# Matmuls of an identity in PE's waits at the openings of a mixture of experts and of an attention

## What is computed

```python
x = x + attention0(layernorm(x), ctx, ctx)            # 16 heads of 16, softmax over 64 keys
x = x + expert_choice_ffn(layernorm(x))               # 8 experts, each takes its top 1024 of 8192 rows
x = x + attention1(layernorm(x), ctx, ctx, masks)     # the same, with a key mask and a pad mask
x = x + zone_ffn(layernorm(x))                        # 8 experts of width 256 on every row, weights by a router
```

## Time and profile before

| what | value |
|---|---|
| median of 3 runs | 2336.3 us (2335.57 to 2337.42) |
| the profiled execution, its own time | 2335.41 us |
| its span, first to last instruction | 2333.3 us |
| mean granted clock of PE | 0.968 of 2.4 GHz |
| PE busy | 2171.5 us, 93% of the span |
| DVE, ACT, POOL busy | 1453.1, 872.9, 361.6 us |
| DMA | 114.00 MB, 49 GB/s on the mean |

### The profile page before, as it was taken

One profiled execution on the slowest core, in us unless ns is written; L12 is line 12 of the kernel. 1 busy time (PEld: TensorE's weight loads), 2 busy tenths in 40 slices (PEclk: granted clock), 3 DMA queues, 4 the chain that ended last, 5 costly groups with the idle time before them and its releaser, 6 DMA issues. The chain is left out here.

```text
span 2333.3 us, 40339 instructions
## 1 busy us (share of the span) xinstructions
PE 2171.5 (93%) x15221; PEld 1855.4 (80%) x15221; DVE 1453.1 (62%) x3169; ACT 872.9 (37%) x1245; POOL 361.6 (15%) x347
## 2 busy tenths in 40 slices
PE   6999998638999769999998999999999999999998
PEld 4888887427898747777777888888888888888887
DVE  6888887785555368777776854545545555544444
ACT  2555554124555235555454322222222222222222
POOL 3111110106776411111112100000000000000000
PEclk9999999858999979999999999999999999999999
DMA  3121211104544312112213100000000000000000
GB/s 98 55 72 63 81 63 46 30 3 132 108 102 77 37 37 73 63 54 72 81 64 127 37 15 14 28 28 28 28 28 28 1 28 28 28 28 28 28 10 10
DMA packets 109098, 114.00 MB, mean 49 GB/s; under 512 B 16064, under 2 KB 97728, under 8 KB 108992
## 3 DMA queue, kind: packets, MB, share of 16 engines
q1 hardware_dynamic: 96704, 95.44, 12.8%
q0 software_dynamic: 12288, 17.05, 4.5%
HBM read 61.87 MB, written 50.59 MB: 48 GB/s over the span
## 5 line engine op out<-in xcount | busy, mean ns | idle before, releaser
L2224 DVE TENSOR_TENSOR zmix_hid<-zmix_act_gate,psum 128x1024 f32<-128x1024 f32 x128 | 156.3, 1221 | 378.6 <-issue 350.8
L2180 ACT ACTIVATE zmix_hid_hi<-zmix_hid 128x1024 fp32r<-128x1024 f32 x128 | 135.6, 1059 | 393.6 <-PE psum L144 232.5
L2172 ACT ACTIVATE zmix_act_gate<-psum 128x1024 f32<-128x1024 f32 x128 | 131.4, 1027 | 377.4 <-PE psum L144 377.3
L752 PE MATMUL psum<-att_v_cur,att_probs 128*128 128x96 f32 x2048 | 247.9, 277 | 3.1 <-ACT att_probs L911 3.1
L752 PEld LDWEIGHTS psum<-att_v_cur,att_probs 128*128 128x128 f32 x2048 | 238.1, 192 | 10.9 <-ACT att_probs L911 4.0
L2229 DVE TENSOR_TENSOR zmix_hid_lo<-zmix_hid,zmix_hid_hi 128x1024 fp32r<-128x1024 f32 x128 | 157.8, 1233 | 134.9 <-ACT zmix_hid_hi L2180 133.9
L142 PE MATMUL psum<-zmix_wd_hi,zmix_hid_hi 128*128 128x256 f32 x768 | 217.3, 283 | 2.2 <-DVE zmix_acc L2215 1.9
L143 PE MATMUL psum<-zmix_wd_lo,zmix_hid_hi 128*128 128x256 f32 x768 | 217.2, 283 | 0.0
L144 PE MATMUL psum<-zmix_wd_hi,zmix_hid_lo 128*128 128x256 f32 x768 | 217.1, 283 | 0.0
L2215 DVE SCALAR_TENSOR_TENSOR zmix_acc<-psum,opened_weight,zmix_acc 128x256 f32<-128x256 f32 x512 | 211.7, 476 | 1.6 <-PE psum L144 1.6
L911 ACT ACTIVATE att_probs<-psum 128x512 f32<-128x512 f32 x256 | 132.2, 604 | 144.4 <-PE psum L731 73.7
(11 more groups left out here) (395 smaller groups left out, 5445.2 us busy)
## 6 DMA issues: line engine op xcount, KB each, us to landing
x<-att_x_new SPq DMA_DIRECT2D x32, 512.0 KB, 2.9
att_x_in<-in_x SPq DMA_DIRECT2D x16, 512.0 KB, 3.8
rows<-att_normed_new SPq DMA_DIRECT2D x16, 512.0 KB, 3.0
att_x_in<-x SPq DMA_DIRECT2D x16, 512.0 KB, 3.8
turned<-att_newT SPq DMA_DIRECT2D x16, 512.0 KB, 2.8
zmix_acc<-x SPq DMA_DIRECT2D x16, 512.0 KB, 4.1
out_x<-zmix_acc SPq DMA_DIRECT2D x16, 512.0 KB, 3.2
moe_wd<-in_w_down SPq DMA_DIRECT2D x8, 768.0 KB
```

Source lines behind the costliest of these rows:

```text
L752: m = pe.matmul(psum[:, 6 + t % 2, cols], probs[:, j, t * P:(t + 1) * P], v_cur[:, p, cols], start=True, stop=True)
L2172: act.activation(act_gate[:, :, :], psum[:, 0:2, :], ACT.Silu).then_inc(gate_out, 1)
L2180: act.activation(hid_hi[:, e % 2, :, :], hid[:, :, :], ACT.Copy).then_inc(hi_made, 1)
L2224: dve.tensor_tensor(hid[:, :, :], act_gate[:, :, :], psum[:, 2:4, :], ALU.mult).then_inc(up_out, 1)
```

## The change

A helper issues `times` matmuls of `ident16` against itself, repeated to 512 columns, into bank 7. Nothing reads what they write, and they wait for nothing and signal nothing. It is called at four places of PE's stream: 42 and 10 times at the mixture, 28 times and twice 8 times (a call in a loop of two) at attention 1.

```diff
+def keep_running(pe, const, psum, times):
+
+    for _ in range(times):
+        pe.matmul(psum[:, 7, :], const["ident16"][:, :], const["ident16"][:, :].unsqueeze(1).to_broadcast([P, TT, P]), start=True, stop=True)
@@ attention, PE's stream, the branch of the second attention
             else:
                 pe.wait_ge(cleared, 2)
+                keep_running(pe, const, psum, 28)
                 turn_input(0, 0)
                 pe.wait_ge(mask_ready, 2)
                 masks(0)
                 queries(0, 0)
                 for c in range(KC):
                     maxima(0, 0, c)
+                    keep_running(pe, const, psum, 8)
                 turn_maxima(0)
             batches(pe, body, close)
@@ expert_choice_mixture, PE's stream
+            keep_running(pe, const, psum, 42)
             turn(0, 0, 0)
+            keep_running(pe, const, psum, 10)
             iterations(pe, body)
```

## The result

The changed kernel took 2328.86 us (median of 10 runs, 2327.38 to 2333.44), the kernel before 2337.59 us beside it (10 runs, 2334.78 to 2340.96): a ratio of 0.9967, 95% interval 0.9959 to 0.9976, which of 2336 us is 7.7 us less, with 5.6 and 9.6 as the ends (the two medians themselves lie 8.7 apart). A second series of the same two kernels gave 0.9971 (0.9960 to 0.9983). The forecast of 2330.9 us lies 2.0 us above the first median, and that median is 0.4 us under the lower end of the range. The times of one kernel don't lie evenly: of 35 runs of the kernel before in a later series 20 lie at 2331.2 to 2335.5 and 15 at 2336.6 to 2340.6, so a median of ten moves by a microsecond or two with how many of each it got.

The account below looks back on a forecast made before the run. PE was taken to bound the kernel, busy 2171.5 of 2333.3 us; 2.4 us at the mixture and 3.0 at the second attention gave 2336.3 - 5.4 = 2330.9 us, with an 8-in-10 range of 2329.3 to 2335.0.

Parts of the forecast that it names:

- Price of an idle matmul: Each further added 512-column matmul on PE costs 0.42 us at 1.2 GHz and 0.22 us at 2.4 GHz.
- Climb r: Time from the start of PE's added matmuls until its clock rises: 4.8 to 5.8 us, with 3.3 as an end.
- The 42, 0.8 late: Mixture's opening: the 42 matmuls ahead of the first transposes end 0.8 us after the rows PE waits for.
- Transposes 0.9 and the first up projection 2.3: Mixture's opening: at the risen clock the 8 transposes save 0.9 us and the first 12 matmuls 2.3 us.
- Rival 2: Mixture's opening: another engine takes the pace and the up projection's 2.3 us return as waits; gain 3.1, 2333.2 us; chance 0.21.
- Mixture opening: Mixture's opening as a whole: 0.9 + 2.3 - 0.8 = 2.4 us gained, with ends 3.2 and 2.1.
- The 28 not late: Second attention's opening: the 28 matmuls end at 826.1 to 826.6, on the 826.50 of the first transposes, delaying nothing.
- Second attention, 0.9 + 1.3 + 0.5 + 0.3: Second attention's opening: transposes 0.9, masks and maxima 1.3, transposes of the maxima 0.5, first scores 0.3; 3.0 us gained.
- Rival 1: Second attention: the clock falls again after the first 8; gain 4.1 down to 3.3 us, 2332.2 to 2333.0; chance 0.23.
- Rival 3: Both openings: the added matmuls do not raise the clock and overrun by 11.9 us in all, 2348.2 us; chance 0.06.
- The sum, 5.4 us: Whole kernel: 2.4 us at the mixture plus 3.0 at the second attention, counted from the median of 2336.3.
- the term for the spread of the runs: Whole kernel: 1 us allowed in the forecast's own range, 2329.4 to 2332.0, for a spread of 1.9 us between runs.

Follow-up runs that it names:

- closes: Changed kernel with idle matmuls also at the closes of both attentions and the zone mixture's start: 2325.09 us, ratio 0.9961 to the kernel before.
- changed_again: The changed kernel measured once more, with no edit, beside the kernel before: 2330.85 us against 2335.88, ratio 0.9971.
- mixture_only: Changed kernel with only the 42 and 10 at the mixture kept, none at the second attention: 2330.09 us, ratio 0.9975 to the kernel before.
- attention_12_4: Changed kernel with 12 and 4 idle matmuls instead of 8 and 8 at the second attention: 2329.8 us, ratio 0.9983 to the kernel before.
- one_column: Changed kernel with each of the 96 added matmuls cut from 512 columns to one: 2334.31 us against 2333.89 for the kernel before, ratio 1.0006.
- attention_28_only: Changed kernel with only the 28 before the second attention's first transposes kept: 2332.77 us, ratio 0.9992 to the kernel before.
- mixture_36: Changed kernel with 36 instead of 42 idle matmuls ahead of the mixture's first transposes: 2331.46 us, ratio 0.9978 to the kernel before.
- mixture_84: Changed kernel with 84 instead of 42 idle matmuls ahead of the mixture's first transposes: 2338.92 us, ratio 1.0008 to the kernel before.
- mixture_10_only: Changed kernel with only the 10 between the mixture's first transposes and first up projection kept: 2332.07 us, ratio 0.9993 to the kernel before.

## Why the prediction was right, and where not

- *Price of an idle matmul, 0.22 warm and 0.42 cold: right.* Ten warm take 2.32 us, 84 take 20.30 with the rise after 4.1 us: 4.1 / 0.42 = 10 cold and 74 at 0.22 make 20.4.
- *Climb r of 4.8 to 5.8 us, with 3.3 as an end: taken too long.* 5.9 and 4.4 us in the changed kernel, 3.4 and 4.3 in its second profiled execution, 4.1 with the 84. Over all 17 groups of 28, 36, 42 or 84 that were profiled it is 2.7 to 5.9 us, 3.9 on the mean, and under 4.8 in 15.
- *The 42, 0.8 late: too much on the mean.* They are 1.06 us late in the changed kernel's first execution and 1.1 in closes, where the rows came 1.2 us sooner after the start of the stage, and on time in changed_again, mixture_only and attention_12_4: 0.4 on the mean of the five.
- *Transposes 0.9 and the first up projection 2.3: right.* 1.97 - 1.04 = 0.93, and 5.06 - 2.86 = 2.2.
- *Rival 2: right in kind, small in size.* PE waits for ScalarE at 548.99, and of the 2.1 us gained by 549.25 (in times of the trace before) in the first execution 0.8 are gone by 574.34; in the second 0.7 of 3.2. The rival had put it at 2.3. In mixture_only, attention_12_4 and closes, which have no such wait there, 0.3 are gone, as in one_column and attention_28_only, where the change doesn't act; in mixture_36 nothing. Mixture opening over the five executions with 42 in front of warm transposes (changed twice, mixture_only, attention_12_4, closes): (1.3 + 2.4 + 2.8 + 2.8 + 2.9) / 5 = 2.4 us, as predicted. That it comes out so close is in part luck: the lateness was 0.4 us too high in the sum, and the 0.5 us given back on the mean were put at nothing in it.
- *The 28 not late: right,* with 0.42 us to spare.
- *Second attention, 0.9 + 1.3 + 0.5 + 0.3: right when the clock holds.* In the five executions with 8 and 8 where it does, the start times show 0.84 to 0.90 us gained from the transposes to the queries (0.9 predicted), 1.31 from the second masks to the transposes of the maxima (1.3), and 0.85 to 0.87 from there to the second queries (0.5 + 0.3). Second attention over the six executions with 8 and 8: (2.4 + 2.9 + 3.2 + 3.0 + 3.1 + 2.9) / 6 = 2.9 us, predicted 3.0.
- *Rival 1: it came once.* The maxima lost 0.36 us and the second 8, cold for most of 3.16 us, went past the wait, as its text says; that opening gave 2.4 instead of 2.9 to 3.2, a loss of 0.6 where the rival had 1.3 to 2.1, since the clock fell only after the masks. PE's idles before that fall were 0.78 and 1.81 us; with 0.78 and 1.78 us in changed_again it didn't fall. The trace agrees here with the rule cited in the prediction from the Trainium skill ("TensorE: Matmul & The Clock Gate", section "A second HAM failure mode: psum-queue depth-cycling"): short idles between groups were enough, in one execution of six.
- *Rival 3: excluded,* as the rises show; mixture_84 shows what such a length would have cost.
- *The sum, 5.4 us: right.* 2.4 + 2.9 = 5.3 by the traces. By the times it may be somewhat more: the interval of the first series begins at 5.6 us, just above it, that of the second (4.0 to 9.3) holds it, and the four series of kernels that fill all these waits and no others (the changed one twice, mixture_36, attention_12_4) have ratios of 0.9967, 0.9971, 0.9978 and 0.9983, on the mean 0.9975, or 5.9 us of 2336.
- *What failed is the term for the spread of the runs.* I gave it 1 us, from three runs that lay within 1.9. The runs of the kernel before went from 2331.14 to 2340.96 later. That term should have been 2 to 3 us at each end; the lower end of the range missed the measured time for want of it. Not the mechanism, but the number of the time itself hangs on it: 2330.9 counted from a median of three, and the second series' median of the same changed kernel is 2330.85.

What stays open: why executions of one kernel spread over 4 to 10 us. Waits of PE for ScalarE in the mixture's loop (0.3 us idle and some 0.5 us lost each) and a fall of the clock at the close of attention 1 come in some profiled executions and not in others and add up to several microseconds, but no run here set them one by one.

## What to carry to other kernels

Where PE waits long and then does work that others wait for, at half clock, matmuls that nobody reads buy that work back; look for such places by the granted clock in the stage, not by PE's busy share. Count what you fill with against the wait, at 0.42 us each while the clock is still down (2.7 to 5.9 us here) and at 0.22 after, since what overruns is paid in full; and put a short group into each wait that follows, or part of the gain goes again. One profiled pair is not a measure of a change of 5 us in 2330: take the openings, stretch by stretch, from several executions, and take the level from many runs.

## What the runs showed of the hardware

- The clock's rise after the start of dense work isn't fixed: 3.4 and 5.9 us for the same 42 matmuls in two executions of the same kernel, 2.7 us (28 matmuls, attention_12_4) to 5.9 over all, and 3.4 and 8.8 us after the start of cold transposes in mixture_10_only, where ten idle matmuls follow them, and one_column, where a wait follows.
- Forty-two matmuls of one column (1.26 us in all) did not bring the clock up: it rose at 542.00, and without them at 543.06, with the stage 0.4 us later. How a longer train of such matmuls would do, no run shows.
- Twelve microseconds of matmuls into a bank that nobody reads delayed no other engine by an amount that shows: in the changed kernel DVE's copy of the gates, which the rows' transfer releases, starts at 533.30, where PE got the rows at 533.64 before and the stage lies 0.3 us earlier, and DVE's step for the low parts takes 1.22 us, before 1.23.
